# GpSimd makes the near mask of the attention distances too, in place of VectorE

## The chip, the cores and the metric

The kernel runs on one core of a Trainium2 chip. The metric is the device time of one execution in microseconds, lower is better. The kernel before took 247.17 us, the median of 3 runs (246.69 to 248.42).

## The reference

One decoder layer over x of 8 batches, 128 positions and 128 features: layer norm and attention, layer norm and a gated cross part over a context, layer norm and a mixture of 8 experts (the best 2 for each row), each added to x. The change lies in the attention, which scores by a distance and not by a product:

```
diff_sq = maximum(|q|^2 - 2 q.k + |k|^2, 0);  ed = sqrt(diff_sq + 1e-8);  ns = |q|^2 + |k|^2
dist = where(ed < 0.1, dist_taylor,                       # near
       where(ed > 2.0, 0.693 + log(ed + 1e-8) + c*ns/4,   # far
             ed * sqrt(1 + c*ns)))                        # between
attn = softmax(causal(-beta * dist));  o = attn @ v       # 16 heads of 8 features
```

## The kernel before, in words

Every engine has its own list of instructions and waits for the others by semaphores. The attention is cut into 16 units; a unit is one batch and half of its heads, as a tile of 128 rows by 640 columns (the causal part of the scores in strips). All engines go through the units in steps. In step s each does a fixed sequence of pieces of work, which belong to several units at once, so that the units overlap like stages of a pipeline.

A unit's way through the engines, by the names in the code (lines are those of the profile of the kernel before):

- TensorE makes the squared distances in P1 and the sums of norms in P2 (`scores`). It may overwrite P2 for the next unit only when the near selection of the unit before is done.
- ScalarE (`step` in its block) takes P1 through a Relu into `e2` (L782), then a logarithm of it `l1` (L787), and squares P2 into `sqn` and `wt` (L799, L807).
- VectorE makes the near mask `m_ge`, one byte for each element, from `e2` (L1142): (e2 + 1e-8) >= 0.01. `far_argument` (L1071) makes `da`; `near_selection` (L1078) puts P2 into `wt` where `m_ge` is set; `product` (L1084) multiplies `e2` and `wt`.
- ScalarE takes the logarithm of the product (L761) and the exponential (L771): that is `dist`.
- GpSimd makes the far mask `m_gt` from `e2` (L602). VectorE's `far_selection` (L1092) puts `da` into `dist` where `m_gt` is set.
- GpSimd adds the causal blocks onto `dist` (L591, L594), after the far selection of the unit. VectorE takes row minima of it (`lowest`, L1101, L1105, L1109).
- TensorE turns `dist` and adds the shift, ScalarE takes the exponential (L751), TensorE multiplies with v, and VectorE divides (L1049, L1053, L1057) and adds to x (L1063).

In the trace `e2`, `l1`, `wt`, `da` and the product all bear the name `dist_mem`, since they share one piece of memory.

The masks have two buffers each, one for even and one for odd units, and so has `e2`. Besides the steps, GpSimd spreads v into other layouts, four copies each after step 0 and step 2 (L627, L628). After the attention it works for the other two parts of the layer; VectorE has work of the next part woven into steps 9 to 13.

In step s the list of GpSimd holds the causal addition of unit s-1 and then the far mask of unit s+1. VectorE's list holds far argument, near selection, minima and product, the near mask of unit s+1, and the far selection of unit s-1.

Of the kernel before, what the change touches and what calls it, by code (L numbers as in the profile page):

```python
# [51 lines left out]
LN_EPS, ATT_EPS, HEAD_EPS = 1e-5, 1e-8, 1e-6  # L52
# [28 lines left out]
def strip_of(t, strip):  # L81

    if strip == 3:
        return t[:, 0:256].rearrange("p (j n) -> p j n", j=2)
    if strip == 1:
        return t[:, 512:640].rearrange("p (j n) -> p j n", j=2)
    two = t[:, 256:512].rearrange("p (j n) -> p j n", j=2)
    return two[:, :, 0:96] if strip == 2 else two[:, :, 96:128]
# [61 lines left out]
def decoder_layer(nc, x, ctx, ctx_t, wq_t, wk_t, wv_t, wo_t, log_c, log_beta, gates_k, gates_b,  # L150
# [4 lines left out]
    ALU, ACT, AX = mybir.AluOpType, mybir.ActivationFunctionType, mybir.AxisListType  # L155

    es = ExitStack()
    with es:  # L158
        def sb(name, shape, dt=fp32):
            return es.enter_context(nc.sbuf_tensor(name, shape, dt))  # L160

        def over(old, shape, dt=fp32, at=0):

            n = int(np.prod(shape[1:]))
            axes = " ".join("abcd"[:len(shape) - 1])
            flat = old[0:shape[0], at:at + n]
            flat = flat if dt == fp32 else flat.bitcast(dt)
            return flat.rearrange(f"p ({axes}) -> p {axes}", **dict(zip("abcd", shape[1:])))

        def sem(name):  # L170
            return es.enter_context(nc.semaphore(name))
# [63 lines left out]
        e2 = over(dist_mem, [128, 2, UW])  # L235
# [6 lines left out]
        m_ge = sb("m_ge", [128, 2, UW], u8)  # L242
# [67 lines left out]
        sm = {n: sem(n) for n in names}  # L310
# [40 lines left out]
        def wait(eng, name, n):  # L351

            if n is None or (isinstance(n, int) and n <= 0):
                return
            eng.wait_ge(sm[name], n)

        def pass_waits(eng):

            eng.sem_inc(sm["passed"], 1)
# [193 lines left out]
        def _(pool):  # L553
# [20 lines left out]
            for c in range(NCH):  # L574
                for s in range(2):
                    pool.wait_ge(sm["split_c"], 2 * c + s + 1)
                    first_mid, low = ((3, 5), (2, 0))[s]
# [2 lines left out]
            pool.wait_ge(sm["cf_in"], 16)  # L580

            def step(s):
                g = s - 1
                if g.there():

                    wait(pool, "dist_done", g.n(1))
                    row = dist[:, g.k % 4, :]
                    cm = cf[:, C_CM:C_CM + ST]
                    cm2 = cm.unsqueeze(1).broadcast_to([128, 2, ST])
                    ends = row[:, 256:512].rearrange("p (j n) -> p j n", j=2)[:, :, 64:128].rearrange("p j (q n) -> p j q n", q=2)  # L590
                    pool.tensor_tensor(ends, ends, cm.unsqueeze(1).unsqueeze(1).broadcast_to([128, 2, 2, ST]), ALU.add)  # L591
                    for strip in (3, 1):
                        end = strip_of(row, strip)[:, :, strip * ST:(strip + 1) * ST]
                        last = pool.tensor_tensor(end, end, cm2, ALU.add)  # L594
                    last.then_inc(sm["causal_done"], 1)
                g = s + 1
                if g.there():

                    wait(pool, "e2_done", g.n(1))
                    wait(pool, "dist_done", g.n(-1))  # L600
                    pass_waits(pool)
                    pool.tensor_scalar(m_gt[:, g.k % 2, :], e2[:, g.k % 2, :], 4.0 - ATT_EPS, None,  # L602
                                       ALU.is_gt).then_inc(sm["gt_done"], 1)
# [341 lines left out]
        def _(dve):  # L945
            link = linker(dve, "chain_d")
            V = dve
# [90 lines left out]
            def at(s, place):  # L1038
                stages = dict(front=front, back=back, stat=stat, late=late)
                for stage, *which in DVE_AT.get((s, place), ()):  # L1040
                    stages[stage](*which)

            def taken(t):
                wait(dve, "pv_done", t.n(1))
                bl = t.k % 2
                if bl:
                    wait(dve, "o_done", t.batch())
                o = PO[:, bl * 144:(bl + 1) * 144].rearrange("p (h n) -> p h n", n=DH + 1)
                V.tensor_copy(o_sb[:, :, :], o).then_inc(sm["o_copied"], 1)  # L1049

            def inverted(t):
                dve.wait_ge(sm["o_copied"], t.batch(1))
                V.reciprocal(o_rec[:, :], o_sb[:, :, DH]).then_inc(sm["o_rec_done"], 1)  # L1053

            def divided(t):
                dve.wait_ge(sm["o_rec_done"], t.batch(1))
                V.tensor_tensor(o_n[:, t.k % 2, :, :], o_sb[:, :, 0:DH],  # L1057
                                o_rec[:, :].unsqueeze(2).broadcast_to([128, H, DH]), ALU.mult).then_inc(sm["o_done"], 1)
# [7 lines left out]
            def far_argument(s):  # L1066
                p = s.k % 2
                wait(dve, "l1_done", s.n(1))
                wait(dve, "sqn_done", s.n(1))
                wait(dve, "dist_done", s.n(-1))  # L1070
                V.scalar_tensor_tensor(da[:, p, :], l1[:, p, :], 2.0, P2f, ALU.mult, ALU.add).then_inc(sm["da_done"], 1)  # L1071

            def near_selection(s):
                p = s.k % 2
                wait(dve, "ge_done", s.n(1))
                wait(dve, "wt_done", s.n(1))
                pass_waits(dve)
                V.copy_predicated(wt[:, p, :], m_ge[:, p, :], P2f).then_inc(sm["sel_done"], 1)  # L1078

            def product(s):  # L1080
                p = s.k % 2
                wait(dve, "sel_done", s.n(1))
                wait(dve, "lp_done", s.n(-1))
                V.scalar_tensor_tensor(prod[:, p, :], e2[:, p, :], ATT_EPS, wt[:, p, :], ALU.add,  # L1084
                                       ALU.mult).then_inc(sm["prod_done"], 1)
# [8 lines left out]
            def lowest(low, part):  # L1094
                if part == 0:
                    wait(dve, "causal_done", low.n(1))
                    d = dist[:, low.k % 4, :]
                    wait(dve, "nmT_full", low.n(-1))
                    m = nm[:, low.k % 2, 0, :].rearrange("p (s j) -> p s j", j=2)
                    for strip in (3, 2, 1, 0):  # L1100
                        last = V.tensor_reduce(m[:, strip, :], strip_of(d, strip), AX.X, ALU.min, negate=True)  # L1101
                    last.then_inc(sm["nm0_done"], 1)
                if part == 1:
                    wait(dve, "nm0_done", low.n(1))
                    V.tensor_tensor(nm[:, low.k % 2, 1, :], nm[:, low.k % 2, 0, :], nm_top[:, low.k % 2, 0:8],  # L1105
                                    ALU.subtract).then_inc(sm["nm1_done"], 1)
                if part == 2:
                    wait(dve, "nm1_done", low.n(1))
                    V.tensor_tensor(nm[:, low.k % 2, 2, :], nm[:, low.k % 2, 1, :], nm_top[:, low.k % 2, 8:16],  # L1109
                                    ALU.subtract).then_inc(sm["nm_done"], 1)  # L1110

            def step(s):
                k_ = s.k
                low, far, near = s - 2, s - 1, s + 1
                t = s - 4
                if t.ends_batch():
                    taken(t)
                if s.there():
                    far_argument(s)
                at(k_, 1)  # L1120
                if s.there():
                    near_selection(s)
                if t.ends_batch():
                    inverted(t)
                at(k_, 2)
                if low.there():
                    lowest(low, 0)
                at(k_, 3)
                if s.there():
                    product(s)  # L1130
                if t.ends_batch():
                    divided(t)
                at(k_, 4)
                if low.there():
                    lowest(low, 1)
                t = s - 5
                if t.ends_batch():
                    residual(t)
                if near.there():
                    wait(dve, "e2_done", near.n(1))  # L1140
                    wait(dve, "sel_done", near.n(-1))
                    V.tensor_scalar(m_ge[:, near.k % 2, :], e2[:, near.k % 2, :], ATT_EPS, 0.01, ALU.add,  # L1142
                                    ALU.is_ge).then_inc(sm["ge_done"], 1)
                at(k_, 5)
                if low.there():
                    lowest(low, 2)
                at(k_, 6)
                if far.there():
                    far_selection(far)
                at(k_, 7)  # L1150
# [747 lines left out]
```

## Time and profile before

| | value |
|---|---|
| median of 3 runs | 247.17 us |
| the profiled execution | 249.05 us, of which the traced span is 246.5 us |
| VectorE busy | 189.1 us (77% of the span) |
| ScalarE busy | 157.6 us (64%) |
| GpSimd busy | 112.2 us (46%) |
| TensorE busy | 196.2 us (80%) |
| units of the attention | about 32 us to 117 us of the span |
| near masks on VectorE | 16, median 0.485 us |
| far masks on GpSimd | 16, median 1.807 us |

The shares are means over the whole span. The attention's steps are read from the order in time of each engine in the stretch 32 to 117 us; there the start of one instruction to the start of the next on the same engine says what it costs the engine, since neighbours overlap by some 0.08 us.

### The profile page before, as it was taken

The page shows a single profiled execution, that of the slowest core. Times are in us where ns is not written, and L with a number is a line of the kernel's source. Part 1 is how long each engine was busy: PE and PEld are TensorE (multiplying, and loading weights), DVE is VectorE, ACT ScalarE, POOL GpSimd, SP SyncE. Part 2 cuts the span into 40 slices and gives each one's busy share as a digit, 9 for nine tenths or more (in the row PEclk, how much of TensorE's full clock was granted, in tenths as well). Part 3 has the DMA queues.
Part 4 walks back from the last instruction along what each step waited for, and adds up shares of the span by engine and source line. Part 5 has one row for each costly group of instructions (what it writes and reads, how often), then busy time and mean ns, then how long its engine had stood idle before and what let it go on. Part 6 is the DMA issues. An engine that isn't in the chain of part 4 may idle for free. (4 is left out here: it accounts for less than half of the span.)

```text
span 246.5 us, 6372 instructions
## 1 busy us (share of the span) xinstructions
PE 196.2 (80%) x2330; PEld 152.0 (62%) x2330; DVE 189.1 (77%) x532; ACT 157.6 (64%) x319; POOL 112.2 (46%) x151
## 2 busy tenths in 40 slices
PE   0797343668687787698899967989999998999994
PEld 0363132456465565487666535578889887898884
DVE  5889879999999999999787488382877844656554
ACT  2499969999999998876436453362555758332320
POOL 9830345694656444636960600130577556643000
PEclk9999955575959657755579996897999999999999
DMA  4304584867285069300030000000000000100001
GB/s 124 92 2 111 162 213 119 225 156 191 70 280 180 11 180 338 87 3 3 1 162 13 1 0 0 0 0 3 0 3 3 0 3 0 43 1 3 0 0 44
DMA packets 28251, 17.41 MB, mean 71 GB/s; under 512 B 11572, under 2 KB 26300, under 8 KB 27964
## 3 DMA queue, kind: packets, MB, share of 16 engines
q1 hardware_dynamic: 28220, 17.01, 24.7%
q8 instruction: 18, 0.29, 0.5%
q14 instruction: 13, 0.11, 0.1%
HBM read 12.03 MB, written 4.92 MB: 69 GB/s over the span
## 5 line engine op out<-in xcount | busy, mean ns | idle before, releaser
L1391 DVE SCALAR_TENSOR_TENSOR dist_mem<-P,gub,dist_mem 128x512 f32<-128x512 f32 x32 | 23.7, 749 | 25.3 <-ACT dist_mem L882 25.0
L882 ACT ACTIVATE dist_mem<-P,gub 128x512 f32<-128x512 f32 x32 | 21.8, 687 | 30.8 <-PE P L1496 30.8
L602 POOL TENSOR_SCALAR m_gt<-dist_mem 128x640 uint8<-128x640 f32 x16 | 29.2, 1824 | 6.9 <-issue 5.0
L1496 PE MATMUL P<-cf,dist 128*128 128x128 f32 x80 | 24.1, 384 | 8.1 <-ACT shift L766 8.1
L1496 PEld LDWEIGHTS PO<-proj_mem,dist_mem 128*128 128x128 f32 x244 | 29.4, 192 | 1.0
L1496 PE MATMUL PO<-proj_mem,dist_mem 128*128 128x128 f32 x244 | 30.0, 276 | 0.0
L1496 PE MATMUL P<-xhi,whi 128*128 128x512 f32 x64 | 27.2, 425 | 1.2 <-DVE dist_mem L1391 1.1
L652 POOL TENSOR_TENSOR wlo<-wgu,whi 128x512 fp32r<-128x512 f32 x16 | 20.9, 1307 | 15.1 <-DVE xn L1001 12.1
L1496 PE MATMUL P<-xlo,whi 128*128 128x512 f32 x64 | 25.7, 402 | 0.0
L1496 PE MATMUL P<-xhi,wlo 128*128 128x512 f32 x64 | 25.6, 400 | 0.0
L1496 PEld LDWEIGHTS P<-cf,dist 128*128 128x128 f32 x80 | 15.5, 194 | 13.3 <-ACT shift L766 10.4
L591 POOL TENSOR_TENSOR dist<-dist,cf 128x128 f32<-128x128 f32 x16 | 7.3, 457 | 33.7 <-DVE dist L1092 33.7
L1496 PE MATMUL P<-shift,cb 128*128 128x128 bf16 x80 | 21.6, 283 | 0.0
L1496 PE MATMUL P<-stn,stq 128*32 128x256 bf16 (+3 forms) x256 | 11.1, 320 | 11.5 <-DVE dist_mem L1078 11.5
L660 POOL TENSOR_TENSOR ctx_sb<-ctx_sb,dist_mem 128x512 f32<-128x512 f32 x8 | 10.4, 1299 | 20.7 <-ACT dist_mem L890 20.7
L1496 PEld LDWEIGHTS P<-stn,stq 128*32 128x32 bf16 x256 | 7.5, 125 | 15.4 <-issue 14.8
L751 ACT ACTIVATE proj_mem<-P,nbeta 128x640 f32<-128x640 f32 x16 | 12.6, 786 | 6.2 <-PE P L1496 6.2
L647 POOL CAST whi<-wgu 128x512 fp32r<-128x512 f32 x16 | 9.8, 613 | 14.1 <-PE P L1496 14.1
L1496 PE MATMUL PO<-vab,proj_mem 128*32 128x9 f32 (+1 forms) x896 | 14.3, 195 | 2.0 <-ACT proj_mem L751 1.2
L1496 PEld LDWEIGHTS PO<-vab,proj_mem 128*32 128x32 f32 x896 | 13.0, 136 | 4.2 <-issue 2.4
L1101 DVE TENSOR_REDUCE nm<-dist 128x2 f32<-128x256 f32 (+1 forms) x64 | 15.4, 303 | 0.0
L1496 PEld LDWEIGHTS P<-xhi,whi 128*128 128x128 f32 x64 | 12.4, 194 | 3.7 <-issue 1.2
(267 smaller groups left out, 516.0 us busy)
## 6 DMA issues: line engine op xcount, KB each, us to landing
q_split<-split_mem SPq DMA_DIRECT2D x16, 128.0 KB, 2.5
k_split<-split_mem SPq DMA_DIRECT2D x4, 512.0 KB, 3.6
stq<-q_split SPq DMA_DIRECT2D x16, 128.0 KB
stk<-k_split SPq DMA_DIRECT2D x16, 128.0 KB
split_mem<-no_rows SPq DMA_DIRECT2D x1, 1024.0 KB, 6.6
wgu<-gate_w SPq DMA_DIRECT2D x1, 1024.0 KB, 5.8
wgu<-up_w SPq DMA_DIRECT2D x1, 1024.0 KB, 9.8
dist<-no_rows SPq DMA_DIRECT2D x1, 1024.0 KB, 4.6
```

The costliest lines, as they stand in the source:

```text
L591: pool.tensor_tensor(ends, ends, cm.unsqueeze(1).unsqueeze(1).broadcast_to([128, 2, 2, ST]), ALU.add)
L602: pool.tensor_scalar(m_gt[:, g.k % 2, :], e2[:, g.k % 2, :], 4.0 - ATT_EPS, None, ALU.is_gt).then_inc(sm["gt_done"], 1)
L647: pool.tensor_copy(hi, w).then_inc(sm["whi_done"], 1)
L652: pool.tensor_tensor(lo, w, hi, ALU.subtract).then_inc(sm["w_ready"], 1)
L660: pool.tensor_tensor(chunk(acc, 0), chunk(acc, 0), yw[:, :, :], ALU.add).then_inc(sm["added"], 1)
L751: A(pT[:, t.k % 2, :], P3f, ACT.Exp, scale=nbeta[:, :]).then_inc(sm["pT_done"], 1)
L882: A(sil[:, f, :], (P1, P2)[f][:, 0, :], ACT.Silu, bias=gub[:, 0, one:one + 1]).then_inc(sm["sil_done"], 1)
L1101: last = V.tensor_reduce(m[:, strip, :], strip_of(d, strip), AX.X, ALU.min, negate=True)
L1391: V.scalar_tensor_tensor(hT[:, z % 2 * 2 + f, :], (P1, P2)[f][:, 1, :], gub[:, 1, one:one + 1], sil[:, f, :], ALU.add, ALU.mult).then_inc( ...
L1496: return nc.tensor.matmul(out_, lhsT, rhs, start=start, stop=stop, **more)
```

## The change

GpSimd makes the near mask of unit s+1 as the first thing in its step s, ahead of the causal addition of unit s-1 and the far mask of unit s+1. VectorE no longer makes it. The operation is the same, with its two arithmetic stages, and so are the two waits (for `e2` of the unit, and for the near selection two units back, which frees the buffer) and the semaphore that is raised. Nothing else is moved.

```diff
@@ -580,6 +580,13 @@
             pool.wait_ge(sm["cf_in"], 16)
 
             def step(s):
+                g = s + 1
+                if g.there():
+
+                    wait(pool, "e2_done", g.n(1))
+                    wait(pool, "sel_done", g.n(-1))
+                    pool.tensor_scalar(m_ge[:, g.k % 2, :], e2[:, g.k % 2, :], ATT_EPS, 0.01, ALU.add,
+                                       ALU.is_ge).then_inc(sm["ge_done"], 1)
                 g = s - 1
                 if g.there():
 
@@ -1111,7 +1118,7 @@
 
             def step(s):
                 k_ = s.k
-                low, far, near = s - 2, s - 1, s + 1
+                low, far = s - 2, s - 1
                 t = s - 4
                 if t.ends_batch():
                     taken(t)
@@ -1136,11 +1143,6 @@
                 t = s - 5
                 if t.ends_batch():
                     residual(t)
-                if near.there():
-                    wait(dve, "e2_done", near.n(1))
-                    wait(dve, "sel_done", near.n(-1))
-                    V.tensor_scalar(m_ge[:, near.k % 2, :], e2[:, near.k % 2, :], ATT_EPS, 0.01, ALU.add,
-                                    ALU.is_ge).then_inc(sm["ge_done"], 1)
                 at(k_, 5)
                 if low.there():
                     lowest(low, 2)
```

GpSimd's list from the second spreading of v on (names: `vab` is v spread, `dist_mem` is `e2`). Before:

```order
L628 COPY vab<-vab 64x4x4x8
L591 TENSOR_TENSOR dist<-dist,cf 128x2x64
L594 TENSOR_TENSOR dist<-dist,cf 128x2x32 x2
L602 TENSOR_SCALAR m_gt<-dist_mem 128x640
L591 TENSOR_TENSOR dist<-dist,cf 128x2x64
```

With the change (lines below the edit are 7 higher):

```order
L635 COPY vab<-vab 64x4x4x8
L588 TENSOR_SCALAR m_ge<-dist_mem 128x640
L598 TENSOR_TENSOR dist<-dist,cf 128x2x64
L601 TENSOR_TENSOR dist<-dist,cf 128x2x32 x2
L609 TENSOR_SCALAR m_gt<-dist_mem 128x640
L588 TENSOR_SCALAR m_ge<-dist_mem 128x640
```

Each turn of GpSimd has one more instruction over 128x640 elements, and it stands between the far mask of one step and the causal addition of the next.

VectorE's list over one step without extra work, from the product to the near selection. Before:

```order
L1084 SCALAR_TENSOR_TENSOR dist_mem<-dist_mem 128x640
L1105 TENSOR_TENSOR nm<-nm 128x8
L1142 TENSOR_SCALAR m_ge<-dist_mem 128x640
L1109 TENSOR_TENSOR nm<-nm 128x8
L1092 COPY_PREDICATED dist<-m_gt,dist_mem 128x640
L1071 SCALAR_TENSOR_TENSOR dist_mem<-dist_mem,P2 128x640
L1078 COPY_PREDICATED dist_mem<-m_ge,P2 128x640
```

With the change:

```order
L1091 SCALAR_TENSOR_TENSOR dist_mem<-dist_mem 128x640
L1112 TENSOR_TENSOR nm<-nm 128x8
L1116 TENSOR_TENSOR nm<-nm 128x8
L1099 COPY_PREDICATED dist<-m_gt,dist_mem 128x640
L1078 SCALAR_TENSOR_TENSOR dist_mem<-dist_mem,P2 128x640
L1085 COPY_PREDICATED dist_mem<-m_ge,P2 128x640
```

The mask is gone from between the two small subtractions of the minima; the rest stands as it was.

## Rows read from the trace of the kernel before

**Rows 1.** The page, part 1: busy time of each engine, its share and instructions.

```profile
PE 196.2 (80%) x2330; PEld 152.0 (62%) x2330; DVE 189.1 (77%) x532; ACT 157.6 (64%) x319; POOL 112.2 (46%) x151
```

**Rows 2.** Busy time by stretch: stretch and length, then each engine, granted clock, DMA.

```profile
62.00:74.00 12.00, 9.01 (x212) 7.03 (x212) 11.69 (x31) 11.64 (x21) 7.10 (x12) 0.74 0.60 179
```

**Rows 3.** VectorE in order of time, one step: start, duration, instruction.

```profile
57.12 0.82 DVE L1071 SCALAR_TENSOR_TENSOR dist_mem<-dist_mem,P 128x640 f32<-128x640 f32 x1
57.86 0.88 DVE L1078 COPY_PREDICATED dist_mem<-m_ge,P 128x640 f32<-128x640 uint8 x1
...
60.33 0.49 DVE L1142 TENSOR_SCALAR m_ge<-dist_mem 128x640 uint8<-128x640 f32 x1
60.73 0.16 DVE L1109 TENSOR_TENSOR nm<-nm 128x8 f32<-128x8 f32 x1
60.81 0.87 DVE L1092 COPY_PREDICATED dist<-m_gt,dist_mem 128x640 f32<-128x640 uint8 x1
...
61.82 0.82 DVE L1071 SCALAR_TENSOR_TENSOR dist_mem<-dist_mem,P 128x640 f32<-128x640 f32 x1
```

**Rows 4.** ScalarE in order of time, around the same step.

```profile
57.73 0.68 ACT L782 ACTIVATE dist_mem<-P 128x640 f32<-128x640 f32 x1
...
61.83 0.72 ACT L771 ACTIVATE dist<-lp 128x640 f32<-128x640 f32 x1
...
65.17 0.74 ACT L761 ACTIVATE lp<-dist_mem 128x640 f32<-128x640 f32 x1
...
66.59 0.72 ACT L771 ACTIVATE dist<-lp 128x640 f32<-128x640 f32 x1
```

**Rows 5.** GpSimd in order of time; idle time before a row and its releaser in brackets.

```profile
57.48 0.60 POOL L594 TENSOR_TENSOR dist<-dist,cf 128x64 f32<-128x64 f32 x2
58.16 1.81 POOL L602 TENSOR_SCALAR m_gt<-dist_mem 128x640 uint8<-128x640 f32 x1
61.77 0.46 POOL L591 TENSOR_TENSOR dist<-dist,cf 128x128 f32<-128x128 f32 x1 [1.79 <-DVE dist L1092]
...
62.87 1.81 POOL L602 TENSOR_SCALAR m_gt<-dist_mem 128x640 uint8<-128x640 f32 x1
```

**Rows 6.** VectorE in order of time: the product one step later.

```profile
64.32 0.81 DVE L1084 SCALAR_TENSOR_TENSOR dist_mem<-dist_mem 128x640 f32<-128x640 f32 x1
```

**Rows 7.** GpSimd in order of time: its first mask, and the first spreading of v.

```profile
33.31 2.00 POOL L602 TENSOR_SCALAR m_gt<-dist_mem 128x640 uint8<-128x640 f32 x1 [4.98 <-issue]
...
37.90 0.54 POOL L627 COPY vab<-vab 96x256 f32<-96x256 f32 x1
...
38.95 0.29 POOL L628 COPY vab<-vab 64x128 f32<-64x128 f32 x1
```

**Rows 8.** VectorE in order of time: near selections of unit 4 and unit 13.

```profile
53.16 0.86 DVE L1078 COPY_PREDICATED dist_mem<-m_ge,P 128x640 f32<-128x640 uint8 x1
...
99.42 0.88 DVE L1078 COPY_PREDICATED dist_mem<-m_ge,P 128x640 f32<-128x640 uint8 x1
```

**Rows 9.** Groups by line and shape, whole span: count, busy us, mean ns, idle before.

```profile
L652 POOL TENSOR_TENSOR wlo<-wgu,whi 128x512 fp32r<-128x512 f32 x16 | 20.9, 1307 | 15.1 <-DVE xn L1001 12.1 <-POOL whi L647 3.0
...
L647 POOL CAST whi<-wgu 128x512 fp32r<-128x512 f32 x16 | 9.8, 613 | 14.1 <-PE P L1496 14.1
```

**Rows 10.** GpSimd in order of time: a mask and a copy beside VectorE's work.

```profile
36.03 1.81 POOL L602 TENSOR_SCALAR m_gt<-dist_mem 128x640 uint8<-128x640 f32 x1 [0.71 <-ACT dist_mem L782]
...
51.43 0.97 POOL L628 COPY vab<-vab 64x128 f32<-64x128 f32 x1
```

**Rows 11.** VectorE in order of time: the instructions beside those two.

```profile
36.28 1.14 DVE L1084 SCALAR_TENSOR_TENSOR dist_mem<-dist_mem 128x640 f32<-128x640 f32 x1
37.35 0.83 DVE L1142 TENSOR_SCALAR m_ge<-dist_mem 128x640 uint8<-128x640 f32 x1
...
51.43 0.87 DVE L1092 COPY_PREDICATED dist<-m_gt,dist_mem 128x640 f32<-128x640 uint8 x1
```

**Rows 12.** VectorE in order of time: work of the next part within step 13.

```profile
104.59 1.62 DVE L1001 TENSOR_SCALAR xn<-x_sb,mv,rs 128x128 f32<-128x128 f32 x4
```

## The prediction

> **What bounds the kernel now.** I read the busy shares first, then busy time by stretch, then each engine in order of time inside the attention. Over the whole span GpSimd looks free, 46% against VectorE's 77% [rows 1]. In a stretch of the attention VectorE is busy 11.69 of 12 us and ScalarE 11.64, GpSimd 7.10 [rows 2]. So both are nearly full there, and GpSimd has about 4.9 us of 12 to give, or 2 us in a step.
>
> In order of time the step is 4.70 us for VectorE (L1071 from 57.12 to 61.82) [rows 3] and 4.76 for ScalarE (L771 from 61.83 to 66.59) [rows 4], in steps without extra work. ScalarE's L761 starts at 65.17, 0.04 after VectorE's product ends (64.32 + 0.81) [rows 4, 6]: ScalarE is paced by VectorE there, while VectorE itself has almost no gap. Over nine steps, from unit 4's near selection at 53.16 to unit 13's at 99.42, the step is 46.26 / 9 = 5.14 us [rows 8]: some steps carry VectorE's division, residual and statistics. VectorE bounds the attention, with ScalarE close behind: taking work from VectorE pays at most the distance to ScalarE.
>
> GpSimd's own turn: causal addition from 61.77 to the far mask at 62.87, 1.10 us, then the mask, 1.81, then 1.79 us or more of waiting for VectorE's far selection [rows 5].
>
> **The change, part by part.**
>
> *VectorE loses the near mask.* It costs the engine 0.40 us a unit (60.33 to the next start at 60.73) [rows 3]. What VectorE would then need is 5.14 - 0.40 = 4.74 us a step, which is ScalarE's 4.76 without extras. Counting some outputs on ScalarE, I take 4.85 as the least step that this can give: 0.29 less than 5.14.
>
> *GpSimd gains it.* The near mask with two arithmetic stages is not in the trace on GpSimd. The nearest row is the far mask: same input, same output type, same size, one stage, 1.81 us [rows 5]. Lower bound: the cast of 512 columns in 0.613 us [rows 9], by columns 0.77 us for 640. Upper bound: the second stage costs as much as the first with everything around it, 3.62 us. The subtraction of two tensors, 1.307 us for 512 [rows 9], gives 1.63 for 640: a real arithmetic stage on two inputs is cheaper than the mask, so what makes the mask dear is not the count of stages. I take 1.81.
>
> GpSimd's turn is then 1.10 + 1.81 + 1.81 and 0.08 between instructions (58.08 to 58.16 [rows 5]) = 4.80 us. From an engine with 2 us of slack it becomes one as full as the other two.
>
> *The order.* Both masks need only `e2`, which for the mask made at 60.33 is ready at 58.41 (57.73 + 0.68) [rows 4]. The near mask goes behind the far mask of the step before, which ends at 59.97, and takes until 61.78 [rows 5]; the near selection that needs it comes one step after 57.86, at 62.56 [rows 3]: slack 0.8. The causal addition behind it starts at 61.78, where it starts now (61.77). So in a lone steady step nothing is late, but every delay of GpSimd beyond 0.8 us reaches VectorE.
>
> *Filling the pipeline.* From its first mask at 33.31 [rows 7] to the end of unit 4's near mask, GpSimd now has nine masks (16.3 us), two causal additions (2.2) and two spreadings of v of 1.34 us each (37.90 to 39.24 [rows 7], 2.7), 21.2 in all: 54.5 us. Unit 4's near selection starts at 53.16 now [rows 8]. **+1.3 us**. This was hidden by idle time of GpSimd; that cover is gone.
>
> *Waits for each other.* At 51.43 a copy on GpSimd started together with VectorE's far selection; it took 0.97 us where its like took 0.29 [rows 7, 10, 11]. At 36.28 VectorE's product, 0.25 us behind the start of a GpSimd mask, took 1.14 instead of 0.81 [rows 6, 10, 11], and a near mask at 37.35, within the same GpSimd mask, 0.83 instead of 0.49 [rows 3, 10, 11]. So the two engines hold each other up, when VectorE reads two tensors of SBUF or makes its mask. In a steady step now GpSimd's mask (62.87 to 64.68) has no such start to fear: it begins beside the near selection. The added mask would begin at 64.68, in the middle of the product (64.32 to 65.13): a wait of 0.45 us [rows 5, 6]. If GpSimd falls behind, its start slides towards the far selection, 0.87 long, and meets that. I take 0.45 a step; the ends are 0 and 0.87. In the four steps of the filling: **+1.8 us**.
>
> *The nine steps from unit 4 to 13.* GpSimd 4.80 + 0.45 = 5.25 against 5.14: **+1.0 us**.
>
> *The last two units.* There VectorE has the next part's rows to normalise within a step, 1.62 us and smaller pieces around it [rows 12]; GpSimd waits again, and VectorE keeps its 0.40 a unit: **-0.8 us**.
>
> Sum: 1.3 + 1.8 + 1.0 - 0.8 = **+3.3 us**. The profiled execution took 249.05 us and so would take 252.35. It lies 1.9 above the median; against 247.17 the forecast is **250.5 us**. What follows the attention moves as a whole and costs nothing more: GpSimd is free again there, and the first blocks of the next part come from VectorE's and ScalarE's end.
>
> **The rivals.** About 1% (2.5 us) is what a measurement can tell from no change: 244.7 and 249.6.
>
> *The second stage is dear.* The mask costs between 2.0 and 3.6 us. GpSimd then bounds every step, and each 0.1 us costs 14 times 0.1 (5 in the filling, 9 behind it). At 2.2 us: 3.3 + 5.5 = +8.8, 256 us; at 3.62: +28.6. For it: it is the one price never seen. Against it: the argument of the subtraction above. 0.24.
>
> *No waits at the shared access, price as taken.* Then GpSimd needs 4.80 and all three engines are level. The nine steps could give 9 x 0.29 = 2.6; I take half, 1.3, since the steps with extra work on one engine are not those of another. 1.3 - 1.3 - 0.8 = -0.8: 246.4 us, no change. 0.18.
>
> *Faster: the near mask streams.* If it costs 0.77 as the cast does, GpSimd's turn is 3.76, the filling ends at 33.31 + 16.0 = 49.3, before 53.16, and VectorE's 0.40 counts until ScalarE binds: 2.6 in the nine steps, 0.8 before them, 0.8 behind: -4.2, 243.0 us. It decides where turn and wait come under 4.85, at a price of 1.4 us. Against it stands the far mask's own 1.81. 0.07.
>
> *The masks shut VectorE out for their whole length.* VectorE's product and far selection would each wait half a mask on average, 0.9 us, behind a GpSimd that is always at a mask: 5.14 - 0.40 + 1.8 = 6.5 a step, +1.4 in some 13 steps, 265 us. The rows speak against it: the product that started at 36.28 was done at 37.42, while the GpSimd mask went on to 37.84, and the product at 64.32 lost nothing under a mask that lasted to 64.68 [rows 5, 6, 10, 11]. 0.05. The Trainium skill (SBUF — State Buffer, "Who interferes with whom") has that rule: whichever of the two starts first has the shared pair for the whole instruction, and the other is blocked fully. By that rule the time would be this rival's. For VectorE's near mask of 37.35 the trace agrees with the rule, for the product it does not.
>
> That a two-stage operation should cost much more is also what the skill speaks against: by GPSIMD Engine Reference, section 3.1, loops of three or more operations run at about three operations a cycle, so one more would be an estimated 0.18 us over 640 columns; the sum would then be 2.5 us higher. No row here shows it.
>
> **How the numbers follow.** Forecast 0.46, dear stage 0.24, no waits 0.18, faster 0.07, whole length 0.05. The forecast's own range is 248 to 253, by waits between 0.1 and 0.65 us a step; a fifth of it lies under 249.6. Slower by over 1%: 0.36 + 0.24 + 0.05 = 0.65. Within 1%: 0.10 + 0.16 = 0.26. Faster: 0.07 + 0.02 = 0.09. The range from 246 to 261 leaves out the streaming mask (0.07), the lower part of the no-wait case (0.04), the whole-length case (0.05) and masks dearer than 2.55 us (0.04), which is 0.20.
>
> **What would show it.** In the profile after: 16 near masks on GpSimd at 1.8 us (right price) or 2.2 and more (the dear rival) or under 1.4 (the faster one). GpSimd busy in nearly the whole attention, the wait of the causal addition for the far selection mostly gone, and in its place VectorE idle ahead of the near selection with GpSimd's mask as releaser, first at unit 2 to 5. Near selection of unit 4 at about 56.3, of unit 13 about 4 us later than 99.42. Some GpSimd masks over 2 us, those that start beside the product or the far selection. The near selections of steps 5.2 to 5.3 us apart. I would be wrong if the selections of units 5 to 13 stood under 5.0 us apart, if VectorE showed no idle time ahead of them, or if GpSimd's masks were all of one length.

## The result

The changed kernel takes 254.91 us (median of 4 runs, 253.90 to 256.55) against 246.96 for the kernel before: a ratio of 1.0297, 95% interval 1.0253 to 1.0341. It is slower by 7.3 us by the ratio. The forecast was 250.5 us, +3.3: right in sign, and the stated range of 246 to 261 us held the time, but the size was 3.3 us where 7.3 were measured. The traced span went from 246.5 to 254.2 us; the traced executions took 249.05 and 256.55 us, each 1.6 to 2.1 us above its median.

The page of the changed kernel, part 1, to be read beside [rows 1]:

```profile
PE 199.3 (78%) x2328; PEld 154.6 (61%) x2330; DVE 190.6 (75%) x516; ACT 158.9 (63%) x319; POOL 149.0 (59%) x167
```

VectorE has 16 instructions fewer and is busy 1.5 us longer: what it was relieved of came back as longer instructions. GpSimd is busy 36.8 us more. The groups of the two masks say where that is (page, part 5: line, operation, count, busy us, mean ns, idle before):

```profile
L588 POOL TENSOR_SCALAR m_ge<-dist_mem 128x640 uint8<-128x640 f32 x16 | 38.0, 2374 | 5.3 <-ACT dist_mem L789 4.3
...
L609 POOL TENSOR_SCALAR m_gt<-dist_mem 128x640 uint8<-128x640 f32 x16 | 29.1, 1817 | 1.3
```

The near mask costs 2.36 us on GpSimd (2.37 in the mean), 0.55 us more than the far mask of the same shape. GpSimd in order of time (start, duration) over one turn, answering to [rows 5]:

```profile
60.44 2.36 POOL L588 TENSOR_SCALAR m_ge<-dist_mem 128x640 uint8<-128x640 f32 x1
62.77 0.46 POOL L598 TENSOR_TENSOR dist<-dist,cf 128x128 f32<-128x128 f32 x1
63.19 0.59 POOL L601 TENSOR_TENSOR dist<-dist,cf 128x64 f32<-128x64 f32 x2
63.86 1.82 POOL L609 TENSOR_SCALAR m_gt<-dist_mem 128x640 uint8<-128x640 f32 x1
65.76 2.36 POOL L588 TENSOR_SCALAR m_ge<-dist_mem 128x640 uint8<-128x640 f32 x1
```

There is no idle time left: one turn is 5.32 us (60.44 to 65.76), and the 1.79 us of waiting for the far selection are gone. VectorE in the same stretch, answering to [rows 3, 6]:

```profile
60.56 1.33 DVE L1099 COPY_PREDICATED dist<-m_gt,dist_mem 128x640 f32<-128x640 uint8 x1
62.02 0.82 DVE L1078 SCALAR_TENSOR_TENSOR dist_mem<-dist_mem,P 128x640 f32<-128x640 f32 x1
62.98 0.88 DVE L1085 COPY_PREDICATED dist_mem<-m_ge,P 128x640 f32<-128x640 uint8 x1
...
64.73 0.82 DVE L1091 SCALAR_TENSOR_TENSOR dist_mem<-dist_mem 128x640 f32<-128x640 f32 x1
65.46 0.16 DVE L1112 TENSOR_TENSOR nm<-nm 128x8 f32<-128x8 f32 x1
65.65 0.17 DVE L1116 TENSOR_TENSOR nm<-nm 128x8 f32<-128x8 f32 x1
65.87 1.34 DVE L1099 COPY_PREDICATED dist<-m_gt,dist_mem 128x640 f32<-128x640 uint8 x1
```

Two things are to be seen. The near selection (62.98) starts 0.18 us after GpSimd's mask ends (62.80): the mask paces it, and does so, 0.17 to 0.18 us behind its end, for all units up to 10. In this step VectorE idles only 0.14 us ahead of it (62.84 to 62.98), because the far selection before it was held up. That far selection, 0.11 to 0.12 us behind the start of a GpSimd mask, takes 1.33 us where it took 0.87. If it runs at its bare 0.87 once it is let in, it began in earnest at 61.02, 0.58 us into the mask: GpSimd shuts it out for the first part of the mask and no longer. Two other instructions give the same point. In the changed kernel a small subtraction at 71.19, 0.12 us into the mask of 71.07, took 0.62 us for 0.17, so it began in earnest 0.57 us into the mask. In the kernel before, the product at 36.28 [rows 10, 11], 0.25 us into its mask, began in earnest at 36.61, 0.58 us into the mask of 36.03.

Where the loss arises in time (starts of VectorE's near selection, last line: the end of the span):

| unit | before | changed | later by |
|---|---|---|---|
| 0 | 35.38 | 35.48 | 0.1 |
| 2 | 43.12 | 45.87 | 2.8 |
| 4 | 53.16 | 57.66 | 4.5 |
| 13 | 99.42 | 105.79 | 6.4 |
| 15 | 112.07 | 118.78 | 6.7 |
| end | 246.5 | 254.2 | 7.7 |

4.5 us are lost while the pipeline fills, 1.9 in the nine steps behind (5.35 us each against 5.14), 0.3 in the last two units, and the last 1.0 behind the attention.

### The profile page after: what moved, and what is told of

Its sections match the earlier page's. It is cut to its first block and busy times, and to the rows that moved or that the text cites. A ratio compares the mean times of both kernels' runs of the same rounds, so it can differ in the third digit from the quotient of the medians.

```text
span 254.2 us, 6371 instructions
## 1 busy us (share of the span) xinstructions
PE 199.3 (78%) x2328; PEld 154.6 (61%) x2330; DVE 190.6 (75%) x516; ACT 158.9 (63%) x319; POOL 149.0 (59%) x167
## 5 line engine op out<-in xcount | busy, mean ns | idle before, releaser
L588 POOL TENSOR_SCALAR m_ge<-dist_mem 128x640 uint8<-128x640 f32 x16 | 38.0, 2374 | 5.3 <-ACT dist_mem L789 4.3
L1498 PE MATMUL P<-cf,dist 128*128 128x128 f32 x80 | 25.1, 396 | 9.7 <-ACT shift L773 9.7
L1498 PE MATMUL P<-shift,cb 128*128 128x128 bf16 x80 | 22.5, 290 | 0.0
L1099 DVE COPY_PREDICATED dist<-m_gt,dist_mem 128x640 f32<-128x640 uint8 x16 | 17.6, 1098 | 0.7 <-ACT dist L778 0.3
L1085 DVE COPY_PREDICATED dist_mem<-m_ge,P 128x640 f32<-128x640 uint8 x16 | 14.0, 874 | 4.7 <-POOL m_ge L588 3.9
L1498 PEld LDWEIGHTS PO<-vab,proj_mem 128*32 128x32 f32 x896 | 13.6, 139 | 4.6 <-issue 2.2
```

What stands on the lines that cost most here:

```text
L588: pool.tensor_scalar(m_ge[:, g.k % 2, :], e2[:, g.k % 2, :], ATT_EPS, 0.01, ALU.add, ALU.is_ge).then_inc(sm["ge_done"], 1)
L1099: V.copy_predicated(dist[:, far.k % 4, :], m_gt[:, far.k % 2, :], da[:, far.k % 2, :]).then_inc(sm["dist_done"], 1)
L1498: return nc.tensor.matmul(out_, lhsT, rhs, start=start, stop=stop, **more)
```

## The experiments

All ratios are against runs of the kernel before on the same chip. "Filling" is the start of unit 4's near selection in the trace, "step" the mean step from unit 4 to unit 13. Each is read from one trace, and already the start of unit 0 differs between traces by up to 0.8 us (34.70 in e1_one_stage, 35.48 in the changed kernel), so a difference in the filling below that says nothing by itself. The diffs are shortened: `[...]` and left-out lines stand for the buffer arguments, signals and waits, which go with the mask wherever it goes.

| kernel | ratio (95%) | filling | step |
|---|---|---|---|
| before | 1 | 53.16 | 5.14 |
| changed | 1.0297 (1.0253 to 1.0341) | 57.66 | 5.35 |
| e1_one_stage | 1.0160 (1.0105 to 1.0215) | 54.79 | 5.28 |
| e2_extra_mask | 1.0368 (1.0312 to 1.0425) | 58.25 | 5.54 |
| e3_no_near_mask | 0.9889 (0.9823 to 0.9955) | 52.26 | 4.93 |
| e4_late_spread | 1.0271 (1.0212 to 1.0331) | 56.45 | 5.48 |
| f1_memset_load | 1.0049 (1.0012 to 1.0087) | 55.10 | 4.87 |
| f2_half_one_stage | 1.0062 (1.0025 to 1.0099) | 52.50 | 5.20 |
| f3_three_one_stage | 1.0009 (0.9975 to 1.0042) | 52.33 | 5.16 |
| g1_one_unit_earlier | 1.0287 (1.0232 to 1.0342) | 55.72 | 5.35 |
| g2_earlier_later_units | 1.0093 (1.0059 to 1.0127) | 52.62 | 5.23 |
| g3_product_first | 1.0151 (1.0092 to 1.0210) | 53.42 | 5.26 |
| g4_earlier_product_first | 1.0024 (0.9994 to 1.0053) | 53.15 | 5.04 |

**e1_one_stage.** The change with the mask in one arithmetic stage.

```diff
-pool.tensor_scalar(m_ge[...], e2[...], ATT_EPS, 0.01, ALU.add, ALU.is_ge)
+pool.tensor_scalar(m_ge[...], e2[...], 0.01 - ATT_EPS, None, ALU.is_ge)
```

> The near mask stays on GpSimd, but in one stage: e2 >= 0.01 - 1e-8 in place of (e2 + 1e-8) >= 0.01. Price theory (the second stage costs GpSimd 0.55 us a mask, and its list is the bound): the near mask takes 1.82 us, GpSimd's turn 4.78 where nothing waits; the near selection of unit 4 about 2.7 us earlier than with the change (near 55.0), the steps from unit 4 to 13 about 5.1 us, the whole 6 to 8 us less than the changed kernel, 247 to 249 us. Shared-access theory (what costs is that GpSimd's masks hold up VectorE's two-tensor instructions, whatever a mask costs): far selections of 1.3 us stay and the time stays above 252 us.

Five masks in the filling take 1.81 us, so the second stage is what costs 0.55. The filling is 2.9 us shorter, near the 2.7 of the price theory. But the step stays at 5.28 and the ratio at 1.016, which on the base of the result is 250.9 us: between the outcomes of the two theories. The trace says why. GpSimd around one of the later masks:

```profile
67.16 2.05 POOL L588 TENSOR_SCALAR m_ge<-dist_mem 128x640 uint8<-128x640 f32 x1
69.56 0.46 POOL L598 TENSOR_TENSOR dist<-dist,cf 128x128 f32<-128x128 f32 x1 [0.34 <-DVE dist L1099]
```

and VectorE beside it:

```profile
66.73 0.81 DVE L1091 SCALAR_TENSOR_TENSOR dist_mem<-dist_mem 128x640 f32<-128x640 f32 x1
67.46 0.80 DVE L1064 TENSOR_TENSOR o_n<-o_sb,o_rec 128x128 f32<-128x128 f32 x1
```

The mask wants to start at 67.16 while the product runs to 67.54; it loses 0.24 us. VectorE's division, next after the product, reads two tensors, finds GpSimd's mask reading, and takes 0.80 us where it took 0.28. GpSimd now waits for VectorE again (0.34). So neither engine is full by itself, and both wait for the other. Each theory had half: the price explains the filling, the shared access the steps.

**e2_extra_mask.** The kernel before, and GpSimd makes the two-stage mask into a spare buffer besides.

```diff
+wait(pool, "e2_done", g.n(1)); wait(pool, "sel_done", g.n(-1))
+pool.tensor_scalar(m_spare[...], e2[...], ATT_EPS, 0.01, ALU.add, ALU.is_ge)
```

> The kernel before, VectorE keeps its near mask, and GpSimd makes the two-stage mask too, first in its turn, into a buffer that nobody reads: only GpSimd's load of the change, without VectorE's relief. Price theory: GpSimd's list is the bound with a turn of 5.32 us, VectorE's 0.40 us hardly counts, and the time is within 1.5 us of the changed kernel, 254 to 256. If VectorE were the bound behind held-up instructions, giving its mask back would cost 0.4 us a unit or more: 260 us or above. A rival: the extra mask has no reader in the loop, so VectorE need not wait for it at once, and the lag goes only through the far mask and the causal addition; then 251 to 254.

1.0368 against 1.0297: GpSimd's load alone costs 9.1 us, a little more than the whole change, and VectorE's relief, which is missing here, would be worth some 1.8 us; the two intervals overlap, so this is not clear of noise. On the base of the result the ratio makes 256.0 us: the upper end of the price theory's 254 to 256, not the 260 or above.

**e3_no_near_mask.** Nobody makes the near mask; the kernel leaves the near branch's choice out.

```diff
+V.memset(m_ge[...], 1).then_inc(sm["ge_done"], 1)
-                if near.there():
-                    V.tensor_scalar(m_ge[...], e2[...], ATT_EPS, 0.01, ALU.add, ALU.is_ge)
```

> The kernel before without any near mask: the mask buffer is set to ones once at the start, and neither engine makes masks; this leaves the near branch's choice out. It measures what VectorE's relief is worth with GpSimd as free as before. By the prediction's term (0.40 us a unit, capped by ScalarE at a step of 4.85): the steps from unit 4 to 13 at 4.85 us and the time about 4 us less than before, 243. If the mask filled a gap between two small dependent subtractions and its removal gives back only 0.15 us a unit: about 1.5 to 2 us less, 245 us, with 0.41 us from the first small subtraction to the far selection.

Without any cost on GpSimd the relief is worth 1.1% or 2.7 us, and the step 0.21 us, between the two expectations. The mask had cost VectorE 0.40 from its start to the next, but it stood between two small subtractions that depend on each other. With it, from the first subtraction to the far selection, it was 0.56 us (60.25 to 60.81 in the trace before). Without it, in this kernel, it is 0.42:

```profile
59.21 0.17 DVE L1106 TENSOR_TENSOR nm<-nm 128x8 f32<-128x8 f32 x1
59.41 0.17 DVE L1110 TENSOR_TENSOR nm<-nm 128x8 f32<-128x8 f32 x1
59.63 0.89 DVE L1093 COPY_PREDICATED dist<-m_gt,dist_mem 128x640 f32<-128x640 uint8 x1
```

In the changed kernel it is 0.41 (65.46 to 65.87 above). In steps without extra work the relief is thus 0.15 us, not 0.40: unit 4 to 5 takes 4.55 us (52.26 to 56.81) against 4.70.

**e4_late_spread.** The changed kernel, second spreading of v after step 6.

```diff
-                if s in (0, 2):
-                    spread(s // 2)
+                if s in (0, 6):
+                    spread(s // 6)
```

> The changed kernel, but the second spreading of v (1.3 us on GpSimd) comes after step 6 and not after step 2, still before its reader. Load theory (GpSimd is full from its first mask to unit 13, so only the sum of its work counts): unit 4's near selection is 1.2 us earlier (56.4), unit 13's the same within 0.3 us, the time unchanged within 1 us. Order theory (what is lost while the pipeline fills is lost by the place of that work, and steady steps have room): unit 13 is 1.2 us earlier too, and the time 1 to 1.5 us less.

Unit 4 comes 1.2 us earlier, unit 13 at 105.77 against 105.79, and the time is the same within its interval (the step of 5.48 in the table holds the four copies that were moved into it). In the changed kernel GpSimd is full from its first mask to unit 13; only the sum of its work counts.

**f1_memset_load.** Nearly as long a piece on GpSimd as in e1, but one that reads nothing. The mask buffer holds ones from the start, so the near branch's choice is left out here too.

```diff
-pool.tensor_scalar(m_ge[...], e2[...], ATT_EPS, 0.01, ALU.add, ALU.is_ge)
+wait(pool, "ge_done", g.n())
+pool.memset(xlo[:, 0:950].bitcast(fp32), 0.0)
+pool.memset(xhi[:, 0:950].bitcast(fp32), 0.0)
```

> The changed kernel with the near mask on GpSimd replaced, at its place and with its waits and its signal, by two memsets of 128x950 that write unused memory and read nothing, about 0.9 us each (by the rows of GpSimd's memsets: 0.95 us for 128x1024, 3.94 for 128x4608), together about 1.85 us; VectorE's mask buffer holds ones from the start. It leaves the near branch's choice out. To be read beside e1_one_stage, whose GpSimd work is as long but reads e2: steps of 5.28 us from unit 4 to 13, 252 us. Shared-access theory (GpSimd's masks at the start of their reading hold up VectorE's two-tensor instructions, and are held up by them): the small subtractions and the division go back to 0.16 and 0.28 us, the step falls to 5.0 to 5.1 and the time to 248.5 to 250. Load theory (only the length of GpSimd's list and its order count): the step stays at 5.2 to 5.3 and the time at 251 to 253.

This tells the two apart. GpSimd around the memsets:

```profile
65.27 1.82 POOL L610 TENSOR_SCALAR m_gt<-dist_mem 128x640 uint8<-128x640 f32 x1
67.14 0.89 POOL L589 MEMSET xlo<- 128x950 f32 x1
67.97 0.89 POOL L590 MEMSET xhi<- 128x950 f32 x1
68.83 0.46 POOL L599 TENSOR_TENSOR dist<-dist,cf 128x128 f32<-128x128 f32 x1
```

and VectorE beside them:

```profile
66.90 0.28 DVE L1066 TENSOR_TENSOR o_n<-o_sb,o_rec 128x128 f32<-128x128 f32 x1
67.11 0.16 DVE L1114 TENSOR_TENSOR nm<-nm 128x8 f32<-128x8 f32 x1
67.30 0.17 DVE L1118 TENSOR_TENSOR nm<-nm 128x8 f32<-128x8 f32 x1
67.52 0.88 DVE L1101 COPY_PREDICATED dist<-m_gt,dist_mem 128x640 f32<-128x640 uint8 x1
```

The same instructions of VectorE as in e1, with GpSimd's list in the same order, take 0.28 and 0.16 us, and the step is 4.87 us and not 5.28. GpSimd's list is not quite as long: a turn without waits is 4.66 us (65.27 to 69.93) where e1 has 4.76 (44.23 to 48.99). So at most 0.1 of the 0.41 us is length, and the rest goes with what GpSimd does in that time. That it is the reading fits the held-up instructions of e1; that a memset is also another kind of instruction than a mask, this run can't separate, and g4 below, with real masks, is the second witness. The step is even below 4.93, that of e3; why is open. The filling is 2.8 us longer than in e3: that is what GpSimd's load costs there.

**f2_half_one_stage, f3_three_one_stage.** The one-stage mask on GpSimd for some units, the rest as before.

```diff
+NEAR_POOL = (7, 8, 9, 10, 11, 12, 13, 14)      # f3: (8, 11, 12)
+                if g.there() and g.k in NEAR_POOL:     # GpSimd, ahead of the causal addition
+                    wait(pool, "ge_done", g.n())
-                if near.there():
+                if near.there() and near.k not in NEAR_POOL:
+                    wait(dve, "ge_done", near.n())
```

> A version meant to be better: VectorE makes the near masks of units 0 to 6 and 15, GpSimd those of units 7 to 14, in one stage; so the pipeline fills as before, and VectorE is relieved in the steps with extra work. Price and load theory: filling as before (unit 4 at 53.2), GpSimd's turn 4.78 in the later steps, under VectorE's; the time 1 to 2 us less than before, 245.5 to 247. Shared-access theory: the eight steps are no shorter than before, since what VectorE saves is lost behind GpSimd's masks; the time as before or up to 1.5 us more.

> As the one before, but GpSimd makes the near masks of units 8, 11 and 12 alone, in one stage, which fall into steps where VectorE has both a division and an addition to x. Load theory: 0.2 to 0.4 us less for each, 0.6 to 1.2 in all, 246.5 to 247.5. Shared-access theory: no difference from before beyond 0.5 us.

The filling is as before in both (17.8 and 17.4 us behind unit 0's near selection, 17.8 before). Still f2 is slower by 0.6% and f3 level: the shared-access theory's outcome. In f2 the masks on GpSimd take 1.95 to 2.06 us (one 2.36), as in e1, and VectorE's division 0.81 us, too.

**g1_one_unit_earlier, g2_earlier_later_units.** One-stage masks, made a unit earlier, between the causal addition and the far mask; g1 for units 2 to 15, g2 for 6 to 14.

```diff
                     last.then_inc(sm["causal_done"], 1)
+                g = s + 2
+                if g.there() and g.k in NEAR_POOL:
+                    wait(pool, "e2_done", g.n(1)); wait(pool, "sel_done", g.n(-1)); wait(pool, "ge_done", g.n())
+                    pool.tensor_scalar(m_ge[...], e2[...], 0.01 - ATT_EPS, None, ALU.is_ge)
                 g = s + 1
```

> GpSimd makes the near masks of units 2 to 15 in one stage, but one unit earlier: in step s, between the causal addition of unit s-1 and the far mask of unit s+1, the near mask of unit s+2. The same load on GpSimd as in e1_one_stage, with more than 2 us from the mask to its use in place of 0.8, and the first of the two masks begins beside VectorE's one-input minima. Lateness theory (a mask that is only just in time costs the steps): the time falls to 249 or below. Shared-access theory: the second mask of the turn still begins 1.8 us later, at VectorE's small two-tensor subtractions or its division, which are held to 0.6 to 0.8 us as before; the step stays at 5.2 to 5.3, the time at 251 to 252.5.

> As the one before, for units 6 to 14 alone; VectorE makes the rest, so that the filling is as before. Lateness theory: better than before by 1 to 2 us. Shared-access theory: as f2_half_one_stage, 0 to 1.5 us more than before.

No gain; g1 is as slow as the two-stage change, slower than I expected by either theory. That a mask came only just in time was not what cost the steps. Part of g1's loss is in the filling, where the near mask now stands before the first far masks and behind it the causal additions come late (waits of g1 from 34 to 60 us: who for whom, us in total, times, longest):

```profile
DVE nm L1109 <- POOL dist L595: 3.6, 2, 2.8
```

In the steps the conflict moved to the other mask. GpSimd in g1:

```profile
72.05 1.81 POOL L602 TENSOR_SCALAR m_ge<-dist_mem 128x640 uint8<-128x640 f32 x1
73.94 2.18 POOL L610 TENSOR_SCALAR m_gt<-dist_mem 128x640 uint8<-128x640 f32 x1
```

VectorE in g1:

```profile
72.78 0.93 DVE L1109 TENSOR_REDUCE nm<-dist 128x2 f32<-128x256 f32 x4
73.63 0.81 DVE L1092 SCALAR_TENSOR_TENSOR dist_mem<-dist_mem 128x640 f32<-128x640 f32 x1
74.36 0.80 DVE L1065 TENSOR_TENSOR o_n<-o_sb,o_rec 128x128 f32<-128x128 f32 x1
```

The near mask, beginning before the minima (one input), has its bare 1.81. The far mask behind it starts within the product and takes 2.18, and the division takes 0.80.

**g3_product_first, g4_earlier_product_first.** VectorE takes the product ahead of the minima; g3 with GpSimd as before, g4 with the GpSimd of g2.

```diff
+                if s.there():
+                    product(s)
                 if low.there():
                     lowest(low, 0)
-                at(k_, 3)
-                if s.there():
-                    product(s)
```

> The control for the next one: the kernel before with VectorE's product ahead of the minima and not behind them, nothing on GpSimd changed. ScalarE's logarithm, which waits for the product, can begin 0.9 us earlier, but the product follows at once on the near selection whose result it reads. Within 1 us of before, either way.

> g2_earlier_later_units with that order on VectorE: the far mask on GpSimd now begins while VectorE takes its one-input minima. Shared-access theory: the small subtractions behind them are held less (0.2 to 0.4 us for 0.5), and this kernel is 1 to 2 us better than g2 and, if g3 is level, 0 to 1.5 us better than before. Load theory: no different from g2 by more than 0.5 us.

The order by itself costs 1.5% or 3.7 us, where I had expected less than 1 us either way; no run says why. With it, relief by GpSimd pays: g4 is 1.3 points or 3 us under g3, and level with before. Not all of the 3 us can be put down to the masks. By the traces 2.2 us lie before unit 15's near selection (111.92 against 114.15) and 1.4 behind it, where the two kernels are the same, and the four executions of g3 had a mean granted clock of 0.813 to 0.836, the six of g4 that are compared 0.833 to 0.847. What the steps show does not rest on that: 5.04 us in g4 against 5.26 in g3 is 0.22, the whole of e3's relief of 0.21. GpSimd in g4:

```profile
73.26 1.83 POOL L602 TENSOR_SCALAR m_ge<-dist_mem 128x640 uint8<-128x640 f32 x1
75.17 1.81 POOL L610 TENSOR_SCALAR m_gt<-dist_mem 128x640 uint8<-128x640 f32 x1
```

VectorE in g4:

```profile
73.97 0.82 DVE L1092 SCALAR_TENSOR_TENSOR dist_mem<-dist_mem 128x640 f32<-128x640 f32 x1
74.72 0.99 DVE L1109 TENSOR_REDUCE nm<-dist 128x2 f32<-128x256 f32 x4
75.74 0.17 DVE L1113 TENSOR_TENSOR nm<-nm 128x8 f32<-128x8 f32 x1
```

Both masks now begin beside work with one tensor of SBUF, and have 1.83 and 1.81; the small subtraction at 75.74, 0.57 us behind the second mask's start, is not held. Four divisions take 0.39 us on average where g2 had 0.80, and 0.28 is the bare time. No version here that still makes the near mask beats the kernel before.

## Why the prediction was wrong in size

**The failed step is the price of the near mask**: "I take 1.81", with the subtraction of two tensors as the reason that a second stage costs nothing. It measured 2.36. The reason was a bad one: an instruction of another kind (two inputs, L652) says nothing of what a second stage adds to this kind. The estimate from the Trainium skill (GPSIMD Engine Reference, section 3.1), 0.18 us for one operation more, is a third of the 0.55 that the runs show. The forecast's own dear case began at 2.0 us and had a chance of 0.24; its +8.8 us at 2.2 was closer than the forecast, but at 2.36 its rule would have given +11.0 (3.3 + 14 x 0.55), too much, because it kept the waits of 0.45 beside the price.

Two errors stood against each other. The price missed 14 x 0.55 = 7.7 us, and the sum held 1.8 + 9 x 0.45 = 5.85 us of waits that GpSimd did not have. That filling and steps came out only 2.3 us short, 4.1 for 6.4, is luck. The stated range held the time only because it was drawn wide for the dear stage: the forecast's own range ended at 253 us.

Term by term, forecast and measured:

- *Filling*: forecast 1.3 for work and 1.8 for waits, 3.1. Measured 4.5. With the true price the work is 1.3 + 5 x 0.55 = 4.05, so the waits were nearly nothing there. One was seen: a copy of v at 41.60 took 0.96.
- *Nine steps*: forecast 5.25 (4.80 and 0.45 of waits), +1.0. Measured 5.35, +1.9. The turn of GpSimd without any wait is 5.32 in the rows above; the forecast's 4.80 and the 0.55 make 5.35. The right sum has the price and no waits. In e1, where the price is what I took, the step is 5.28 and the time 1.6% or 4.0 us over before, for a forecast of 3.3. There the waits are real, and split between both engines (0.24 on the mask, 0.52 on the division).
- *Waits on GpSimd's masks*: forecast 0.45 each; in the changed kernel 14 of 16 near masks show 2.35 to 2.36, two 2.43 and 2.53. Masks of one length were a sign of being wrong by the prediction, and it came within two masks of it. VectorE's idle time ahead of the near selection, another sign, was there at units 0 to 2 (0.42, 0.92 and 2.58 us) and shrank to 0.14 in the steps. The waits fell on VectorE, whose far selection was held in five steps (1.33, 2.50, 1.33, 1.34, 1.34). At 54.08 it took 2.50: GpSimd made four copies, began a mask at 55.14, and let it in only at 55.71 (56.58 less 0.87). With GpSimd as the bound VectorE had the time to lose.

```profile
54.08 2.50 DVE L1099 COPY_PREDICATED dist<-m_gt,dist_mem 128x640 f32<-128x640 uint8 x1
```

- *VectorE's relief*: forecast up to 0.29 a step. e3 shows 0.21, and 2.7 us in all.
- *Last two units*: forecast -0.8. Measured +0.3, and -0.1 in e3 (12.55 us from unit 13 to 15 against 12.65): even the free relief gave nothing there.
- *Behind the attention*: forecast nothing; the trace shows 1.0 us more. From unit 15's near selection to the end the traces of all kernels lie between 133.1 (e2) and 136.2 us (g2), with 134.4 before and 135.4 changed, and in no order with what was changed. The ends go with TensorE's granted clock. In the stretch from 25 to 60 us behind that near selection it was 0.90 of full in e2 (133.1) and 0.76 in g2 (136.2), with 0.85 before and 0.80 changed. But f3 (133.9) and f1 (135.6) both had 0.85, so it explains a part at most. This was not tested and stays open.

Put together by the ratios, with e3, f1, e1 and the changed kernel as a ladder: relief of VectorE alone -1.1%; GpSimd's load of one stage, reading nothing, +1.6%; its reading, +1.1%; the second stage, +1.4%. In us: -2.7, +4.0, +2.7, +3.4, together +7.3 before rounding. Each rung is uncertain by 0.7 to 0.8 points, since it compares runs with intervals of their own, taken on different chips, and the one for reading holds the 0.1 us a step by which f1's list is shorter. The load costs in the filling (52.26 to 55.10), the reading in the steps (4.87 to 5.28), the second stage in the filling again (54.79 to 57.66), since in the steps the full list of GpSimd took the place of the held-up instructions (5.28 to 5.35).

**Right**: that GpSimd's apparent freedom (46%) was 2 us in a step, that the added mask would make it as full as the other two and leave no cover for the filling, that the near selection would wait for the mask, and the sign.

**The whole-length rival** is refuted again: the far selection behind a mask of 2.36 us was shut out for 0.57 us, and the division in e1 (done at 68.26, so begun in earnest at 67.98) until 0.58 us after the mask had begun (67.16 and its 0.24 of waiting). The rule of the Trainium skill (SBUF — State Buffer, "Who interferes with whom") is right on who contends: two-tensor instructions of VectorE against GpSimd's reads, and f1, with memsets that read nothing, bears out that part by the division of 0.28 us and the step of 4.87 us. It is not borne out in "for the whole instruction". The 0.57 us are those of two-tensor instructions alone: VectorE's own mask, at 37.35 [rows 11], took 0.34 us longer although it began 1.32 us into GpSimd's. The prediction called this agreement with the rule; held to the end of that mask at 37.84 it would have lost 0.49, or 0.42 counted from the end of the product before it, so the trace agrees only roughly.

## What to carry to other kernels

An engine that is 46% busy on average may have 2 us in a step of 5: cost a move by its turn in that step, with the instruction in the very form that it will have, stages and all. When the price of a form is in no trace, give it the larger share of the range, not a neighbour's price. When two engines share an access, look at what stands beside the start of each GpSimd instruction that reads, since a start of a read beside a two-tensor instruction costs both, and an order that puts one-input work there takes most of the cost away (a step of 5.04 us in g4, 5.23 in g2). That order can cost as much elsewhere, as g3 shows, so it needs its own control.

## What the runs showed that I had not expected

- GpSimd's comparison of 128x640 float32 into bytes takes 1.81 us in one stage and 2.36 in two; VectorE takes 0.48 in two.
- A GpSimd mask shuts out VectorE's two-tensor instructions for about 0.57 us from its start, whether it lasts 1.81 or 2.36 us. Small ones suffer alike: a division of 0.28 us became 0.80.
- GpSimd instructions one behind the other can shut VectorE out longer than each: 1.63 us at 54.08 in the changed kernel.
- Work between two small dependent VectorE instructions is partly free: the mask of 0.40 us there cost 0.15.
